# Decayed attention with two row buffers and decay products first in each gap; last pass shared by VectorE and GpSimd

## The chip, the cores and the metric

One core of one Trainium2 chip runs the whole program in one launch. The metric is the device time of one execution in microseconds, as the median of several. A core has TensorE (PE in the rows; PEld is its weight load), VectorE (DVE), ScalarE (ACT), GpSimd (POOL) and SyncE (SP), each with a queue of its own that is worked off in order; they wait for each other by semaphores.

## The reference

Four layers work on x of 8 x 512 tokens of width 256. After each layer comes `x = layernorm(x + layer(x))`, without gain or offset.

1. Softmax attention, 16 query heads, 4 key and value heads of 64, with rotary positions.
2. A feed-forward layer with quantized weights.
3. Decayed (linear) attention, 16 query heads over 4 key and value heads of 64, with rotary positions. Scores aren't put through a softmax. They are multiplied by a decay that depends on the head and on the distance of the tokens, and a state of 64 x 64 per head carries what lies before a chunk:

```
scores = einsum('bhtd,bhsd->bhts', qi, ki) * mask
o  = einsum('bhts,bhsd->bhtd', scores, vi) + einsum('bhtd,bhde->bhte', qi * q_dec, kv)
kv = blk_dec * kv + einsum('bhtd,bhte->bhde', ki * k_dec, vi)
```

4. A small attention, then a router that picks 2 of 8 experts for each token, and `x + 0.3 * (weighted sum of the two experts)` with the last layernorm behind it.

## The kernel before, in words

All arithmetic is float32. Where TensorE multiplies by weights, an operand is split into a high and a low part (`hi` and `lo`), and three products are summed.

*Decayed attention* (`decay_attention`, lines 640 to 1142) goes through the 8 batches in a loop. A batch has 512 tokens, four tiles of 128, and the kernel uses chunks of 256 tokens, two a batch. The steps of a batch are: transposes of x (`T`), VectorE's split of them (`XH`, `XL`, lines 965 and 969), projections (`Q`, `KV`, line 110), rotation (`ROT`, line 979, on VectorE, which writes two products side by side into the row buffer `rt`; `Y0` and `Y1`, line 1111, on GpSimd, which add them crosswise; `HI` and `LO`, lines 1116 and 1119, which split the sum into the stack `st`), transposes back (`QT`, `KT`, line 874), score products (`S`, line 893), their multiplication by the decay (`M`, line 1003, "decay product" here), the value product (`A`, lines 905 and 908), the state (`VD` on VectorE, line 992, into `vd`; `KV2` on TensorE, line 916; `KH`, a copy), its use (`IN`, line 924), its scaling and sum (`TM` and `OA`, lines 1009 and 1015), the split of the result (`HA` on ScalarE; `LA` on VectorE, line 1019, or on GpSimd, line 1130), the output projection (`W`, line 933), and the sum with x and the layernorm (`F`, `B`, `G`, `N`, lines 1026 to 1038, with `EPS` and `RSTD` on GpSimd, lines 1134 and 1139).

The order is written out by hand (lines 681 to 737). A round of 24 gaps holds one batch, and steps of the next batch lie ahead in it. `put(gap, engine, step)` places a step. Within a gap each engine's steps stand as they were put, but for a sort: TensorE by `turn`, ScalarE with `HA` first, VectorE with `F` first. A score product writes one of two PSUM banks, and waits until the decay product two before it has read that bank. In the first gap VectorE's order is `XH0 XL0 XH1 XL1 TM0 OA0 M`, and in gaps with a rotation the decay product stands behind it. A rotation (`ROT`) waits until GpSimd's `LO` of the rotation before has read `rt`. `VD` waits for the `KV2` of two groups before, as `vd` has two buffers.

*The last pass* (lines 2283 to 2363) comes when all expert tiles are written to memory. For each of 8 batches SyncE loads the two answers of every token (`y_part(b, 0)`, `y_part(b, 1)`, 128 x 1024 each) and x (`x_part(b)`). GpSimd adds the answers (line 2350), one batch ahead; VectorE makes 2x + sum (line 2287), then statistics (lines 2290 and 2295); GpSimd does four small operations on them (lines 2357 to 2363, `EPS`, the reciprocal root `rstd` by a power, shift and sign); ScalarE normalizes (line 2327) and issues the store.

Of the kernel before, what the change touches and what calls it, by code (L numbers as in the profile page):

```python
# [22 lines left out]
ALU = mybir.AluOpType  # L23
AX = mybir.AxisListType

P = 128
BATCH, SEQ, D = 8, 512, 256
TT = SEQ // P
KD = D // P
HEADS, KVH, HD = 16, 4, 64  # L30
GRP = HEADS // KVH
# [47 lines left out]
def shift(seq, n):  # L79

    return seq[0], seq[1] + n
# [551 lines left out]
def decay_attention(nc, const, x_in, x_out, w_q, w_kv, w_o, rope_tab, near_tab, from_tab, to_tab, name):  # L633
# [6 lines left out]
    with ctx:  # L640
        sb = lambda n, s, dt=F32: ctx.enter_context(nc.sbuf_tensor(f"{name}_{n}", s, dt))
# [3 lines left out]
        HH = HEADS // 2  # L645
# [9 lines left out]
        xth, xtl = (sb(n, [P, KD, SEQ], F32R) for n in ("xth", "xtl"))  # L655
        rt = sb("rt", [P, 2, HH * HD])
        kr = sb("kr", [P, 2, KVW])
# [3 lines left out]
        v = sb("v", [P, 2, TT, KVW])  # L661
        vd = sb("vd", [P, 2, 2, GRP * HD])
        kv = sb("kv", [P, 2, GRP * HD])
# [20 lines left out]
        gaps, ahead_keys = {}, {eng: set() for eng in ENGINES}  # L684
# [45 lines left out]
        for g in range(ROUND):  # L730
            gaps[g, "tensor"] = sorted(gaps.get((g, "tensor"), []), key=lambda k: -2 if k[0] == "W" and k[2] else turn[k[0]])
            gaps[g, "vector"] = sorted(gaps.get((g, "vector"), []), key=lambda k: k[0] != "F")
            gaps[g, "scalar"] = sorted(gaps.get((g, "scalar"), []), key=lambda k: k[0] != "HA")
# [5 lines left out]
        pe_s, dve_s, act_s, pool_s = (S[n] for n in ENGINES[:4])  # L739
# [4 lines left out]
        units = [k for k in order["tensor"] if k[0] in ("Q", "KV")]  # L744
        st_place = {("HI",) + k: n % 2 for n, k in enumerate(units)}
        rt_place = {("ROT",) + k: 0 for k in units}

# [31 lines left out]
        def rows_of(u):  # L779

            heads = HH if u[0] == "Q" else KVH
            line = kr[:, u[1], :] if u[0] == "KV" and u[1] < 2 else rt[:, 0, 0:heads * HD]
            stack = st[:, st_place[("HI",) + u], 0:heads * 2 * HD]
            return heads, line, line.rearrange("p (h d) -> p h d", d=HD), stack.rearrange("p (h d) -> p h d", d=2 * HD)

        with nc.Block() as block:
# [51 lines left out]
            def _(pe):  # L838
# [3 lines left out]
                def steps(i, run):  # L842
                    in_misc = [x for x in misc if x in run or x + (0,) in run]
                    for key in run:
                        kind, j = key[0], own(i, key)
# [8 lines left out]
                        if kind == "T":  # L854
                            k = key[1]
# [54 lines left out]
                        elif kind == "KV2":  # L910
# [3 lines left out]
                            for t in range(2):  # L914
                                for s in range(2):
                                    last = nc.tensor.matmul(m[HD * s:HD * s + HD, 0:GRP * HD], kr[:, t, HD * g:HD * g + HD], vd[:, g % 2, t, :], start=(t == 0), stop=(t == 1))
                        elif kind == "IN":
# [21 lines left out]
            def _(dve):  # L939
# [12 lines left out]
                def steps(i, run):  # L952
                    rot = [k for k in run if k[0] == "ROT"]
                    for key in run:
# [15 lines left out]
                        elif kind == "ROT":  # L970
# [5 lines left out]
                            for seq, k in last_use(i, rot, key, rt_place, ahead["vector"], order["vector"]):  # L976
                                dve.wait_ge(*pool_s.at(seq, "LO", *k[1:]))
                            w = heads * HD
                            op = vv.tensor_tensor(rt[:, :, 0:w].rearrange("p u (h d) -> p u h d", d=HD),  # L979
                                                  ps_m[:, bank[u], 0:w].rearrange("p (h d) -> p h d", d=HD).unsqueeze(1).broadcast_to([P, 2, heads, HD]),  # L980
# [6 lines left out]
                        elif kind == "VD":  # L987
                            g = key[1]
                            dve.wait_ge(*pool_s.at(j, "VV", 0))
                            dve.wait_ge(tables_in, 32)  # L990
                            dve.wait_ge(*(pe_s.at(j, "KV2", g - 2) if g >= 2 else pe_s.at(shift(j, -1), "KV2", g + 2)))
                            op = vv.tensor_tensor(vd[:, g % 2, :, :].rearrange("p t (h d) -> p t h d", d=HD),
                                                  v[:, 1, 0:2, HD * g:HD * g + HD].unsqueeze(2).broadcast_to([P, 2, GRP, HD]),
# [99 lines left out]
            def _(pool):  # L1093
# [3 lines left out]
                def steps(i, run):  # L1097
                    hi = [k for k in run if k in st_place]
                    for key in run:
                        kind, j = key[0], own(i, key)  # L1100
                        u = key[1:]
                        if kind in ("Y0", "Y1", "HI", "LO"):
                            heads, line, rows, stack = rows_of(u)
                            half = lambda x, c: x.rearrange("p (h c d) -> p h c d", c=2, d=HALF)[:, :, c, :]
                            a, b = rt[:, 0, 0:heads * HD], rt[:, 1, 0:heads * HD]
                        if kind in ("Y0", "Y1"):
# [907 lines left out]
def sparse_experts(nc, const, x_in, by_expert, answers, bias_parts, counts, raw, staged, w, x_out, name):  # L2014
# [6 lines left out]
    with ctx:  # L2021
# [70 lines left out]
        with nc.Block() as block:  # L2092
# [120 lines left out]
            def _(dve):  # L2213
# [69 lines left out]
                for b in range(BATCH):  # L2283
                    x = b % RAW
                    dve.wait_ge(staged[x], 16 * (len(pieces) // RAW) + 16 * (b // RAW) + 16)
                    dve.wait_ge(added, b + 1)
                    vv.scalar_tensor_tensor(out=y_part(b, 1), in0=x_part(b), scalar=2.0, in1=y_part(b, 0), op0=ALU.mult, op1=ALU.add).then_inc(summed, 1)
                    dve.wait_ge(summed, b + 1)
                    for t in range(TT):
                        vv.bn_stats(st6[:, b % 2, t, :], y_part(b, 1)[:, D * t:D * t + D]).then_inc(stats, 1)  # L2290
                    if b >= 2:
                        dve.wait_ge(normed, TT * (b - 1))
                    for t in range(TT):
                        hold(dve, stats, TT * b + t + 1)
                        vv.bn_aggr(mv[:, b % 2, t, :], st6[:, b % 2, t, :]).then_inc(means, 1)
# [37 lines left out]
            def _(pool):  # L2333
# [19 lines left out]
                for b in range(BATCH):  # L2353
                    if b + 1 < BATCH:
                        add(b + 1)
# [116 lines left out]
```

## Time and profile before

| | us |
|---|---|
| median of 3 runs | 3228.32 (3227.73 to 3229.99) |
| profiled execution | 3231.17 |
| its span | 3229.4 |
| TensorE busy | 2767.0 (86%) |
| VectorE busy | 1985.2 (61%) |
| ScalarE busy | 1299.3 (40%) |
| GpSimd busy | 1068.6 (33%) |

The span is what the profile of one execution shows, from its first to its last instruction. Decayed attention fills about 1450 to 2127 us of it, the last pass 3170 to the end. The mean granted clock of TensorE over the span is 0.942 of full speed. In a row, "idle before" is how long the engine did nothing ahead of that instruction, and the arrow names what ended it. Columns of the views are named at their first group below.

### The profile page before, as it was taken

What the parts mean: (1) busy time and instruction counts of PE and PEld (TensorE: products, weight loads), DVE (VectorE), ACT (ScalarE), POOL (GpSimd) and SP (SyncE); (2) the same over time, 40 slices, a digit from 0 to 9 for tenths busy, and PEclk for the clock granted to TensorE, in tenths of its full rate; (3) what the DMA queues carried; (4) which work ended last, traced back from release to release, by engine and by line L of the source; (5) the groups of instructions that cost most, each with busy time, mean ns of one, the idle gap of its engine ahead of it and who ended that gap; (6) DMA issues with size and microseconds to landing.
All of it is one profiled execution on the core that took longest, in us unless ns stands there. A gap on an engine that the chain in (4) does not pass through costs nothing. (4 is left out here: it accounts for less than half of the span.)

```text
span 3229.4 us, 62896 instructions
## 1 busy us (share of the span) xinstructions
PE 2767.0 (86%) x17098; PEld 1956.6 (61%) x17099; DVE 1985.2 (61%) x3659; ACT 1299.3 (40%) x2735; POOL 1068.6 (33%) x1446
## 2 busy tenths in 40 slices
PE   6998989999898978877999999969999999809992
PEld 4666666666675647765666666644555555408992
DVE  3656666565666658864555555557777777546664
ACT  2554554545454532212222222215555555424443
POOL 4333343434334311115555555510111111122225
PEclk8999999999999989999999999979999999959996
DMA  2111011111101121112111110022222222052225
GB/s 64 34 31 41 28 38 41 27 38 27 44 24 38 34 80 33 39 70 72 33 32 32 32 32 26 26 67 75 70 65 63 64 64 64 18 172 87 72 74 199
DMA packets 146409, 175.43 MB, mean 54 GB/s; under 512 B 21130, under 2 KB 109730, under 8 KB 145570
## 3 DMA queue, kind: packets, MB, share of 16 engines
q1 hardware_dynamic: 135076, 149.89, 15.9%
q0 software_dynamic: 6912, 18.96, 1.6%
q10 hardware_dynamic: 4224, 4.19, 0.4%
q8 instruction: 94, 1.54, 0.2%
q14 instruction: 103, 0.84, 0.1%
HBM read 90.83 MB, written 37.06 MB: 40 GB/s over the span
## 5 line engine op out<-in xcount | busy, mean ns | idle before, releaser
L560 ACT ACTIVATE soft_probs<-soft_ps_s,soft_mx 128x512 f32<-128x512 f32 x512 | 347.8, 685 | 395.1 <-DVE soft_mx L479 370.4
L479 DVE TENSOR_REDUCE soft_mx<-soft_ps_s 128x1 f32<-128x512 f32 x512 | 329.4, 685 | 236.7 <-PE soft_ps_s L389 224.1
L1817 DVE TENSOR_REDUCE mla_mx<-mla_ps_s 128x1 f32<-128x512 f32 x512 | 334.9, 686 | 133.7 <-PE mla_ps_s L1670 133.2
L1928 ACT ACTIVATE mla_pt<-mla_ps_t 128x512 f32<-128x512 f32 x512 | 289.9, 596 | 265.2 <-PE mla_ps_t L1682 263.1
L389 PE MATMUL soft_ps_s<-soft_ks,soft_qs 128*128 128x512 f32 x1024 | 309.8, 422 | 13.9 <-ACT soft_probs L560 13.9
L398 PE MATMUL soft_ps_p<-ident,soft_probs 128*128 128x128 f32 x2048 | 266.4, 273 | 12.0 <-DVE soft_mx L479 8.5
L398 PEld LDWEIGHTS soft_ps_p<-ident,soft_probs 128*128 128x128 f32 x2048 | 236.7, 141 | 46.7 <-DVE soft_mx L479 10.6
L489 DVE COPY soft_pt<-soft_ps_p 128x512 f32<-128x512 f32 x256 | 175.6, 686 | 138.7 <-PE soft_ps_p L398 134.0
L389 PEld LDWEIGHTS soft_ps_s<-soft_ks,soft_qs 128*128 128x128 f32 x1024 | 171.2, 190 | 147.9 <-issue 59.0
L407 PE MATMUL soft_ps_a<-soft_pt,soft_v 128*64 128x512 f32 x1024 | 251.2, 612 | 0.0
L1670 PE MATMUL mla_ps_s<-mla_stack,mla_pad 128*128 128x512 f32 x512 | 239.4, 474 | 8.8 <-DMA mla_pad<-mla_stack 5.9
L1682 PE MATMUL mla_ps_t<-mla_shifted,mla_pad 128*128 128x512 f32 x512 | 207.1, 407 | 0.2
L979 DVE TENSOR_TENSOR decay_rt<-decay_ps_m,decay_rope 128x1024 f32<-128x1024 f32 (+1 forms) x96 | 100.3, 1045 | 164.1 <-PE decay_ps_m L110 89.9
L567 ACT COPY soft_pt<-soft_ps_p 128x512 f32<-128x512 f32 x256 | 149.8, 585 | 83.0 <-PE soft_ps_p L398 72.3
L1692 PE MATMUL mla_ps_a<-mla_pt,mla_v 128*32 128x256 f32 x2048 | 168.5, 402 | 12.6 <-ACT mla_pt L1928 12.5
L1670 PEld LDWEIGHTS mla_ps_s<-mla_stack,mla_pad 128*128 128x128 f32 x512 | 100.2, 196 | 129.8 <-DVE mla_mx L1817 85.3
L1111 POOL TENSOR_TENSOR decay_rt<-decay_rt 128x256 f32<-128x256 f32 (+1 forms) x160 | 115.1, 740 | 156.3 <-DVE decay_rt L979 156.3
L893 PE MATMUL decay_ps_s<-decay_qs,decay_ks 128*128 128x512 f32 x384 | 138.2, 441 | 32.7 <-DVE decay_pt L1003 32.7
L588 POOL TENSOR_TENSOR soft_rt<-soft_rt 128x256 f32<-128x256 f32 (+1 forms) x192 | 120.2, 648 | 136.5 <-DVE soft_rt L466 136.5
L1067 ACT CAST decay_qs<-decay_ps_m 128x512 fp32r<-128x512 f32 x128 | 70.2, 589 | 185.0 <-PE decay_ps_m L874 184.4
L2344 POOL DMA_INDIRECT answers<-moe_blank,moe_xt x72 | 69.1, 960 | 227.7 <-DVE moe_blank L2265 227.7
L466 DVE TENSOR_TENSOR soft_rt<-soft_ps_m,soft_rope 128x1024 f32<-128x1024 f32 (+1 forms) x96 | 99.6, 1038 | 71.9 <-POOL soft_st L599 38.9
(359 smaller groups left out, 6577.9 us busy)
## 6 DMA issues: line engine op xcount, KB each, us to landing
soft_rrep<-inverse SPq DMA_DIRECT2D x128, 128.0 KB, 2.9
mla_pad<-mla_stack SPq DMA_DIRECT2D x256, 64.0 KB, 2.0
moe_xt<-by_expert SPq DMA_DIRECT2D x72, 129.0 KB, 2.0
soft_ks<-soft_ks SPq DMA_DIRECT2D x64, 128.0 KB, 2.3
decay_ks<-decay_ks SPq DMA_DIRECT2D x64, 128.0 KB, 2.4
raw<-in_L_ffn_w SPq DMA_DIRECT2D x16, 512.0 KB, 5.4
mla_stack<-mla_yh SPq DMA_DIRECT2D x128, 64.0 KB, 2.1
soft_xc<-in_L_attn_x SPq DMA_DIRECT2D x8, 512.0 KB, 4.3
```

The costliest lines, as they stand in the source:

```text
L389: last = nc.tensor.matmul(ps_s[:, s_bank(n), :], qs[:, h, P * t:P * t + P], ks[:, b, g, :], start=(b == 0), stop=(b == 1))
L398: last = nc.tensor.transpose(ps_p[:, c % 2, P * t:P * t + P], probs[:, h % 2, t, P * c:P * c + P], ident[:, :])
L407: last = nc.tensor.matmul(ps_a[HD * s:HD * s + HD, 0, :], v[:, 1, c, HD * g:HD * g + HD], weights_of(2 * p + s, c), start=(c == 0), stop=( ...
L479: op = vv.tensor_reduce(out=mx[:, h, t:t + 1], in_=ps_s[:, s_bank(4 * h + t), :], axis=AX.X, op=ALU.max, negate=True)
L489: op = vv.tensor_copy(weights_of(h, c), ps_p[:, c % 2, :])
L560: op = nc.scalar.activation(probs[:, h % 2, t, :], ps_s[:, s_bank(4 * h + t), :], ACT.Exp, bias=mx[:, h, t:t + 1], scale=1.0, accum_out=rs ...
L567: op = nc.scalar.copy(weights_of(h, c), ps_p[:, c % 2, :])
L1670: last = nc.tensor.matmul(ps_s[:, (4 * t + s + 16 * a) % S_BANKS, :], pad[:, QUADS + a, s, P * t:P * t + P], stack[:, a, :], start=True, s ...
L1682: last = nc.tensor.matmul(ps_t[:, s % 2, :], pad[:, a, s, P * t:P * t + P], shifted[:, a, :], start=True, stop=True)
L1692: last = nc.tensor.matmul(ps_a[32 * s:32 * s + 32, 0, cols], v[:, t, 4 * a + s, :], pt[:, t % 2, s, cols], start=(t == 0 and half == 0), s ...
L1817: op = vv.tensor_reduce(out=mx[:, a, t, s:s + 1], in_=ps_s[:, (16 * a + 4 * t + s) % S_BANKS, :], axis=AX.X, op=ALU.max, negate=True)
L1928: op = nc.scalar.activation(pt[:, t % 2, s, :], ps_t[:, s % 2, :], ACT.Exp, scale=KPH ** -0.5)
```

## The change

- The row buffer `rt` gets two places. Rotations take them in turn, and each waits for GpSimd's `LO` of the rotation before the last. `vd` goes from two buffers to one, and `VD` waits for the `KV2` of the group just before.
- On VectorE the sort within a gap puts decay products (`M`) first, then `F`, then the rest as put.
- In the last pass GpSimd adds the answers of even batches only. For odd batches VectorE makes 2x + first answer, and then adds the second answer.

```
-        rt = sb("rt", [P, 2, HH * HD])
+        rt = sb("rt", [P, 2, 2, HH * HD])
-        vd = sb("vd", [P, 2, 2, GRP * HD])
+        vd = sb("vd", [P, 2, GRP * HD])
-            gaps[g, "vector"] = sorted(gaps.get((g, "vector"), []), key=lambda k: k[0] != "F")
+            gaps[g, "vector"] = sorted(gaps.get((g, "vector"), []), key=lambda k: {"M": 0, "F": 1}.get(k[0], 2))
-        rt_place = {("ROT",) + k: 0 for k in units}
+        rt_place = {("ROT",) + k: n % 2 for n, k in enumerate(units)}
...
-                            dve.wait_ge(*(pe_s.at(j, "KV2", g - 2) if g >= 2 else pe_s.at(shift(j, -1), "KV2", g + 2)))
+                            dve.wait_ge(*(pe_s.at(j, "KV2", g - 1) if g else pe_s.at(shift(j, -1), "KV2", KVH - 1)))
...
-                    dve.wait_ge(added, b + 1)
-                    vv.scalar_tensor_tensor(out=y_part(b, 1), in0=x_part(b), scalar=2.0, in1=y_part(b, 0), op0=ALU.mult, op1=ALU.add).then_inc(summed, 1)
-                    dve.wait_ge(summed, b + 1)
+                    if b % 2 == 0:
+                        dve.wait_ge(added, b // 2 + 1)
+                        vv.scalar_tensor_tensor(out=y_part(b, 1), in0=x_part(b), scalar=2.0, in1=y_part(b, 0), op0=ALU.mult, op1=ALU.add).then_inc(summed, 2)
+                    else:
+                        dve.wait_ge(tile_in[b], DONE + 32)
+                        vv.scalar_tensor_tensor(out=y_part(b, 0), in0=x_part(b), scalar=2.0, in1=y_part(b, 0), op0=ALU.mult, op1=ALU.add).then_inc(summed, 1)
+                        dve.wait_ge(summed, 2 * b + 1)
+                        vv.tensor_tensor(y_part(b, 1), y_part(b, 0), y_part(b, 1), ALU.add).then_inc(summed, 1)
+                    dve.wait_ge(summed, 2 * b + 2)
...
-                    if b + 1 < BATCH:
+                    if b % 2 and b + 1 < BATCH:
                         add(b + 1)
```

## Rows read from the trace of the kernel before

**Rows 1.** Stretches: bounds, length, busy PE PEld DVE ACT POOL, granted clock, DMA.

```profile
1430.00:2127.00 697.00, 617.85 (x3997) 444.38 (x3995) 391.86 (x618) 143.65 (x259) 362.08 (x499) 0.96 0.13 39
...
1769.80:1773.20 3.40, 3.40 (x24) 2.25 (x22) 0.00 (x0) 1.17 (x2) 0.00 (x0) 0.76 0.00 0
```

**Rows 2.** Waits of PE in 1540:2100: total, times, longest.

```profile
PE decay_ps_s L893 <- DVE decay_pt L1003: 25.4, 25, 2.1
PE decay_ps_m L933 <- POOL decay_atl L1130: 9.5, 7, 1.4
```

**Rows 3.** Waits of DVE in 1540:2100.

```profile
DVE decay_rt L979 <- POOL decay_st L1119: 44.4, 33, 2.4
```

**Rows 4.** Timeline of PE: start, us, what, count, [idle before, releaser]; round's start.

```profile
1764.04 0.66 PE L874 MATMUL decay_ps_m<-ident,decay_st 128*128 128x128 f32 x4 [0.72 <-DVE decay_xtl L969]
1764.45 0.71 PE L893 MATMUL decay_ps_s<-decay_qs,decay_ks 128*128 128x512 f32 x2
1767.28 0.74 PE L893 MATMUL decay_ps_s<-decay_qs,decay_ks 128*128 128x512 f32 x2 [2.12 <-DVE decay_pt L1003]
1767.95 1.08 PE L905 MATMUL decay_ps_a<-decay_pt,decay_v 128*64 128x256 f32 x4
...
1769.38 1.97 PE L874 MATMUL decay_ps_m<-ident,decay_st 128*128 128x128 f32 x8
1771.28 0.93 PE L916 MATMUL decay_ps_m<-decay_vd,decay_kr 128*64 128x256 f32 x6
```

**Rows 5.** Timeline of DVE at the round's start.

```profile
1760.56 1.23 DVE L979 TENSOR_TENSOR decay_rt<-decay_ps_m,decay_rope 128x1024 f32<-128x1024 f32 x1 [2.37 <-POOL decay_st L1119]
...
1762.57 0.69 DVE L965 CAST decay_xth<-decay_ps_m 128x512 fp32r<-128x512 f32 x1 [0.19 <-PE decay_ps_m L859]
...
1766.55 0.68 DVE L1003 TENSOR_TENSOR decay_pt<-decay_ps_s,decay_near 128x512 f32<-128x512 f32 x1
1767.15 0.68 DVE L992 TENSOR_TENSOR decay_vd<-decay_v,decay_from_end 128x512 f32<-128x512 f32 x1
```

**Rows 6.** Timeline of PE, score products in 1776:1788.

```profile
1780.75 0.73 PE L893 MATMUL decay_ps_s<-decay_qs,decay_ks 128*128 128x512 f32 x2 [0.84 <-DVE decay_pt L1003]
...
1785.67 0.74 PE L893 MATMUL decay_ps_s<-decay_qs,decay_ks 128*128 128x512 f32 x2 [0.91 <-DVE decay_pt L1003]
```

**Rows 7.** Timeline of PE in 1812:1826.

```profile
1815.98 1.04 PE L874 MATMUL decay_ps_m<-ident,decay_st 128*128 128x128 f32 x8
...
1817.40 0.65 PE L905 MATMUL decay_ps_a<-decay_pt,decay_v 128*64 128x256 f32 x4
...
1823.10 0.38 PE L933 MATMUL decay_ps_m<-decay_woh,decay_ath 128*128 128x256 f32 x1 [1.36 <-POOL decay_atl L1130]
```

**Rows 8.** Timeline of DVE in 1812:1826.

```profile
1816.06 0.67 DVE L1038 TENSOR_SCALAR decay_xb<-decay_xb,decay_mv,decay_rstd 128x256 f32<-128x256 f32 x1 [1.58 <-POOL decay_rstd L1139]
1816.66 1.21 DVE L979 TENSOR_TENSOR decay_rt<-decay_ps_m,decay_rope 128x1024 f32<-128x1024 f32 x1
```

**Rows 9.** Timeline of POOL at the round's start.

```profile
1767.46 1.50 POOL L1130 TENSOR_TENSOR decay_atl<-decay_ot,decay_ath 128x512 fp32r<-128x512 f32 x1 [1.76 <-ACT decay_ath L1087]
```

**Rows 10.** Timeline of DVE, the next round's first cast.

```profile
1845.17 0.69 DVE L965 CAST decay_xth<-decay_ps_m 128x512 fp32r<-128x512 f32 x1 [0.20 <-PE decay_ps_m L859]
```

**Rows 11.** Timeline of POOL in the last pass.

```profile
3209.28 2.35 POOL L2350 TENSOR_TENSOR moe_w1h<-moe_w1h,moe_w1l 128x1024 f32<-128x1024 f32 x1
...
3212.13 1.75 POOL L2359 TENSOR_TENSOR moe_rstd<-moe_vare,minus_half 128x4 f32<-128x4 f32 x1 [0.18 <-POOL moe_vare L2357]
...
3214.65 2.35 POOL L2350 TENSOR_TENSOR moe_w1h<-moe_w1h,moe_w1l 128x1024 f32<-128x1024 f32 x1
...
3220.72 1.04 POOL L2359 TENSOR_TENSOR moe_rstd<-moe_vare,minus_half 128x4 f32<-128x4 f32 x1 [0.18 <-POOL moe_vare L2357]
```

**Rows 12.** Timeline of DVE in the last pass, one batch.

```profile
3211.74 1.24 DVE L2287 SCALAR_TENSOR_TENSOR moe_w1l<-moe_w2h,moe_w1h 128x1024 f32<-128x1024 f32 x1 [2.36 <-POOL moe_w1h L2350]
```

**Rows 13.** Stretch near the end of the last pass's loads.

```profile
3208.00:3210.00 2.00, 0.00 (x0) 0.00 (x0) 1.38 (x8) 0.64 (x2) 1.63 (x4) 0.50 0.83 291
```

More of the change, by code:

```diff
@@ L781, in rows_of @@
             heads = HH if u[0] == "Q" else KVH
-            line = kr[:, u[1], :] if u[0] == "KV" and u[1] < 2 else rt[:, 0, 0:heads * HD]
+            line = kr[:, u[1], :] if u[0] == "KV" and u[1] < 2 else rt[:, rt_place[("ROT",) + u], 0, 0:heads * HD]
             stack = st[:, st_place[("HI",) + u], 0:heads * 2 * HD]
@@ L915, in steps @@
                                 for s in range(2):
-                                    last = nc.tensor.matmul(m[HD * s:HD * s + HD, 0:GRP * HD], kr[:, t, HD * g:HD * g + HD], vd[:, g % 2, t, :], start=(t == 0), stop=(t == 1))
+                                    last = nc.tensor.matmul(m[HD * s:HD * s + HD, 0:GRP * HD], kr[:, t, HD * g:HD * g + HD], vd[:, t, :], start=(t == 0), stop=(t == 1))
                         elif kind == "IN":
@@ L978, in steps @@
                             w = heads * HD
-                            op = vv.tensor_tensor(rt[:, :, 0:w].rearrange("p u (h d) -> p u h d", d=HD),
+                            op = vv.tensor_tensor(rt[:, rt_place[key], :, 0:w].rearrange("p u (h d) -> p u h d", d=HD),
                                                   ps_m[:, bank[u], 0:w].rearrange("p (h d) -> p h d", d=HD).unsqueeze(1).broadcast_to([P, 2, heads, HD]),
@@ L990, in steps @@
                             dve.wait_ge(tables_in, 32)
-                            dve.wait_ge(*(pe_s.at(j, "KV2", g - 2) if g >= 2 else pe_s.at(shift(j, -1), "KV2", g + 2)))
-                            op = vv.tensor_tensor(vd[:, g % 2, :, :].rearrange("p t (h d) -> p t h d", d=HD),
+                            dve.wait_ge(*(pe_s.at(j, "KV2", g - 1) if g else pe_s.at(shift(j, -1), "KV2", KVH - 1)))
+                            op = vv.tensor_tensor(vd[:, :, :].rearrange("p t (h d) -> p t h d", d=HD),
                                                   v[:, 1, 0:2, HD * g:HD * g + HD].unsqueeze(2).broadcast_to([P, 2, GRP, HD]),
@@ L1104, in steps @@
                             half = lambda x, c: x.rearrange("p (h c d) -> p h c d", c=2, d=HALF)[:, :, c, :]
-                            a, b = rt[:, 0, 0:heads * HD], rt[:, 1, 0:heads * HD]
+                            place = rt_place[("ROT",) + u]
+                            a, b = rt[:, place, 0, 0:heads * HD], rt[:, place, 1, 0:heads * HD]
                         if kind in ("Y0", "Y1"):
```

## The prediction

> **What bounds the kernel now.** I read the page's slices first, then the stage of decayed attention by stretches, then who waits for whom in it, then one of its rounds engine by engine, and last the pass that ends the kernel. A round is one pass of the stage's loop. It can be timed by the first VectorE cast of a batch: 1762.57 us in one round [rows 5], 1845.17 in the next [rows 10], so 82.6 us. In the stage TensorE is busy 617.85 of 697 us, VectorE 391.86 and GpSimd 362.08 [rows 1]: TensorE sets its length, and only what leaves TensorE idle, or slows its clock, can give time. In the 560 us of six round starts TensorE waited 25.4 us for VectorE's decay products (25 times, the longest 2.1) and 9.5 us for GpSimd's low half of the result (7 times) [rows 2]. The waits of VectorE itself, 44.4 us of rotations for GpSimd [rows 3], cost nothing by themselves. They cost where a decay product stands in VectorE's queue behind them.
>
> One round shows where. (a) The score product at 1767.28 waits 2.12 us [rows 4], because its PSUM bank is freed by a decay product that runs seventh in its gap, at 1766.55, behind two casts, two subtractions, one scaling and one sum that began at 1762.57 [rows 5]. TensorE's work right behind it is slow: four matmuls of 256 columns take 1.08 us where they else take 0.65, eight transposes 1.97 where they else take 1.04 [rows 4, 7]. There the granted clock is 0.76 on the mean of a stretch [rows 1], so it fell to the lower level (1.2 GHz) for a part of it, after the round's longest idle. (b) Two more score products wait 0.84 and 0.91 us for decay products that stand behind rotations [rows 6]. (c) The output projection of tile 2 waits 1.36 us for GpSimd [rows 7].
>
> In the last pass GpSimd is the queue that never rests: per batch an addition of 2.35 us, then four small operations that fill the 3.0 us until the next addition [rows 11]. A batch costs 5.37 us (3209.28 to 3214.65). VectorE and ScalarE idle half of it.
>
> **Part 1: decay products first in each gap (and two row buffers).** No instruction is added, and no duration changes. What changes is order.
>
> At (a) the product at 1766.55 goes ahead of the casts. Its scores were made before the transposes of x, and the queue is free for it: the rotation that now starts at 1760.56 after a wait of 2.37 us for GpSimd [rows 5] no longer waits with a second buffer, and the product behind that one goes ahead of it too. So the casts still start at 1762.57, when their transposes are there, and I cost their delay at nothing (if that cover were missing, 0.6 us, one product). The bank is free early, and TensorE goes on behind the score product of 1764.45: next score product at about 1765.05, value product at 1765.7, transposes at 1766.5 (from start to start 0.67 us as at 1767.28, and 0.8 us for the eight matmuls of a value product), done at 1767.3. Next late are the decayed values `vd`: their multiplication starts where it does now, at 1767.15, and ends at 1767.83 [rows 5], so the state matmuls start at 1767.9 after 0.6 us of idle. They start at 1771.28 now [rows 4]. Of these 3.4 us, the slow clock makes (1.97 - 1.04) + (1.08 - 0.65) and a little more of the same value product [rows 4, 7], about 1.7; the order alone makes 1.7.
>
> At (b) both waits go, 0.84 + 0.91 = 1.75 us [rows 6]. The product that frees the bank for 1785.67 needs the scores begun at 1780.75, 4.9 us earlier, so it has them well before the rotation that now stands ahead of it; the other place is alike. Where a product runs behind a rotation and TensorE doesn't wait, the new order gives nothing.
>
> At (c) the order costs. The chain is: reciprocal root on GpSimd, normalization on VectorE at 1816.06 (it waited 1.58 us for that), rotation at 1816.66 [rows 8], GpSimd's four operations on it, its low half of the result, and then TensorE at 1823.10 [rows 7]. A decay product now steps between normalization and rotation: plus 0.6 us on a path that TensorE waits for. The second row buffer doesn't help here, since the normalization came last, not the buffer.
>
> Sum for a round: 1.7 + 1.75 - 0.6 = 2.85 us. Seven batches are overlapped with a next one and have all these places, so 20 us. Bounds: if nothing but (b) comes, 7 x (1.75 - 0.6) = 8; if the 0.6 us at (c) isn't paid, 7 x 3.45 = 24.
>
> **The clock.** With the idle of 2.12 us gone, the stretch ahead of the fall holds idles of 0.7 and 0.6 us instead of 0.72 and 2.12, and a score and a value product between them. Idles like that occur elsewhere in the round ((b), (c)) and no fall follows them. Nothing in the trace shows where the line is, so I bound it: 0 if it still falls each round, 7 x 1.7 = 12 if it never falls. I take 8, five rounds of seven without it.
>
> **Part 2: one buffer less for `vd`, the buffers themselves.** Each multiplication into `vd` now waits for the state matmuls of the group before, not of two before. In TensorE's order those matmuls stand ahead of scores whose decay product VectorE has to do before that multiplication anyway, so the wait is over when it is reached. Nothing; if it were on the path, about one group of state matmuls, 0.93 us [rows 4], a round. The second row buffer takes most of VectorE's 44.4 us of waits [rows 3] away. What that gives TensorE is in (a) already: the queue is free early there.
>
> **Part 3: the last pass.** Per two batches GpSimd loses one addition (2.35 us), VectorE gains one product of 1.24 us [rows 11, 12] and its queue for an odd batch has two of them in a row. The cycle that ends last is then: addition for the even batch, VectorE's product and statistics on it (3.0 us), GpSimd's small operations on it, next addition. The small operations last 3.0 us when one VectorE product runs beside them; the root takes 1.75 us beside it and 1.04 alone [rows 11]. Beside two products in a row they last between 3.0 and 4.3. A pair costs 8.5 to 9.8 instead of 10.74. Batches 1 to 6 take 30.6 us now, from statistics to statistics (6 x 5.37 less the part of an addition that is ahead at the start, 1.6), and 3 pairs, 25.5 to 29.4, then. Batch 7 takes two products and statistics, 4.25 us, instead of 5.37. So its root, at 3220.72 now [rows 11], comes 2.3 to 6.2 us earlier. A second bound: the loads still keep the DMA engines 0.83 busy in 3208 to 3210 [rows 13], so batch 7 is not there before about 3209.5, later if the stores come earlier. That cuts the top to about 5. I take 3.5.
>
> The Trainium skill (SBUF — State Buffer, section "Who interferes with whom") says that a VectorE instruction with two SBUF inputs and a GpSimd instruction that reads SBUF exclude each other, and that whichever starts first holds the port for the whole instruction. The root's 1.75 against 1.04 us [rows 11] agrees for the order in which VectorE is first. By that rule alone the long end of the pair, 9.8 us, would hold, and the pass would give 2.3 us instead of 3.5. The same rule speaks against part 1 at one place, which is rival 3.
>
> **Sum.** 20 + 8 + 3.5 = 31.5 us. The profiled execution took 3231.17 us (span 3229.4 and 1.8 around it), 2.9 above the median of the runs, 3228.32. From 3231.17 it gives 3199.7, and as a median 3197.
>
> **Rivals.**
> 1. *The clock still falls each round.* For it: it falls in all rounds now, whatever the length of the rest, and the transposes around 1762 to 1764 stay. Against: the long idle is what this place has and the others don't. Then 20 + 3.5: 3205.
> 2. *The waits move instead of going.* TensorE arrives earlier at rotations' transposes and at GpSimd's results. For it: GpSimd's chain already holds TensorE at (c), VectorE's casts hold it 0.72 us [rows 4]. Against: only 9.5 us of TensorE's waits are for GpSimd's results now [rows 2], so most of them come early. If (b)'s gains are given back and the clock stays as it is, 7 x (1.7 - 0.6) + 3 = 11: 3217.
> 3. *The multiplication into `vd` gets behind GpSimd's subtraction.* They start 0.3 us apart, VectorE first (1767.15 and 1767.46) [rows 5, 9]. If GpSimd were first by a little and VectorE had to wait for its 1.5 us, the state matmuls would start 1.2 us later each round: 8 us less gain, 3205. (The Trainium skill's same section makes this a full block.)
> 4. *Slower.* A decay product in front of every rotation puts 0.6 us before each of the 12 rotations of a round. It decides from the point where GpSimd's lead over the transposes is under 0.6 us: at (c) there is none now. If the lead were gone at all twelve, 7.2 us a round would be lost against 3.9 of idle removed (2.12 + 1.75): 7 x 3.3 less 3.5, 20 us slower: 3248. With half of them it comes out level.
> 5. *The order doesn't do what it says.* The score products would wait for something else (a state copy, a bank of the projections). Then only part 3: 3225.
>
> **How the numbers follow.** Forecast (31.5 us) 0.50; rival 1 0.24; rival 3 or mixtures with rival 1 0.07; rival 2 0.09; rival 5 0.04; rival 4 0.06. A measurement of this kernel tells about 0.2% (6.5 us) from no change. Faster by more than that: 0.50 + 0.24 + 0.07 + 0.09 = 0.90. Within: 0.04 and a part of rival 4, 0.05. Slower: 0.05. The likeliest case alone spans 3187 (24 + 12 + 5) to 3203 (20 + 2 + 3). The range with rivals 1 and 3 and a part of 2 is 3186 to 3213.
>
> **What would show it.** Right: no score product waits over 0.3 us for a decay product; the state matmuls start within 5.5 us of a batch's first cast (8.7 now); rounds of 78 to 80; no rotation waits for GpSimd; the wait at (c) about 2 us; the batches of the last pass 4.3 to 4.9 us apart. Clock: pieces of 8 transposes of 1.97 us missing. Wrong: rounds above 81 us, or a new releaser of the score products.

## The result and the profile after

| | before | after |
|---|---|---|
| median of 4 runs, us | 3228.95 (3227.73 to 3229.99) | 3178.57 (3169.70 to 3181.52) |
| profiled execution, us | 3231.17 | 3180.66 |
| its span | 3229.4 | 3178.9 |
| mean granted clock | 0.942 | 0.945 |

The ratio is 0.9833, 95% interval 0.9821 to 0.9846: 50 us less. The forecast was 3197, range 3186 to 3213. The sign was right, and so was what was said of the places in a round and of the last pass. The gain was put too low, mainly by what the second row buffer gives, and the time lies 7 us under the range.

The stretches show where the time is. The first row answers to [rows 1]; the second and third are one round each, from the first cast of a batch to that of the next. Columns as there.

```profile
1430.00:2080.00 650.00, 601.40 (x4020) 442.73 (x4019) 401.50 (x619) 142.22 (x259) 363.29 (x500) 0.98 0.14 42
1663.72:1740.90 77.18, 73.58 (x498) 54.08 (x497) 49.18 (x77) 17.18 (x32) 44.97 (x62) 1.00 0.12 34
1740.90:1818.03 77.13, 73.54 (x498) 54.08 (x497) 49.20 (x76) 17.18 (x32) 44.97 (x62) 1.00 0.12 34
```

A round took 82.5 to 83.9 us before, 83.02 on the mean of six, and takes 77.2 now. The granted clock is 1.00 in each of them. In the kernel before the clock fell to its lower level (1.2 GHz) once in every round, and two kinds of rounds stood beside each other: a round with the longer fall has a mean granted clock of 0.96, the common one 0.98 (same view):

```profile
1678.76:1762.57 83.81, 77.16 (x498) 55.43 (x497) 48.23 (x77) 17.39 (x32) 44.96 (x63) 0.96 0.11 31
1762.57:1845.17 82.60, 75.94 (x498) 54.84 (x497) 48.11 (x77) 17.38 (x32) 44.96 (x63) 0.98 0.11 32
```

From SyncE's first load of x in decayed attention to its last store of x, right behind the last normalization, it is 695.3 us before (1442.5 to 2137.8) and 642.6 after (1444.3 to 2086.9): 52.7 less. The six rounds make 35.1 of it, what lies before the second batch 6.0 (71.1 to 65.1), what lies behind the last batch's first cast 11.6 (126.1 to 114.5). The last pass is 3.1 shorter. Two other stretches, which the change doesn't touch, are together 5.3 longer: 1.8 ahead of decayed attention, 3.5 between it and the last pass.

The waits of TensorE after, in the six rounds, answer to [rows 2] (total, times, longest):

```profile
PE decay_ps_m L933 <- POOL decay_atl L1131: 10.9, 7, 1.6
PE decay_ps_m L874 <- DVE decay_xtl L969: 4.3, 6, 0.7
PE decay_ps_m L874 <- POOL decay_st L1120: 3.2, 7, 0.5
PE decay_ps_m L916 <- DVE decay_vd L992: 3.1, 6, 0.5
PE decay_ps_m L933 <- DVE decay_rt L979: 2.3, 7, 0.3
```

The waits for decay products, 25.4 us before, are gone. Two new waits have come, on `vd` and on a rotation at the output projection (L933). VectorE's side answers to [rows 3]:

```profile
DVE decay_pt L1003 <- PE decay_ps_s L893: 84.0, 68, 2.9
```

The direction has turned round: the decay products now wait for scores. The waits of rotations for GpSimd, 44.4 us before, are 2.6, in 5 times, the longest 0.5. The round's start, TensorE, answers to [rows 4]:

```profile
1742.78 1.17 PE L893 MATMUL decay_ps_s<-decay_qs,decay_ks 128*128 128x512 f32 x4
1743.88 0.65 PE L905 MATMUL decay_ps_a<-decay_pt,decay_v 128*64 128x256 f32 x4
...
1744.68 1.09 PE L874 MATMUL decay_ps_m<-ident,decay_st 128*128 128x128 f32 x8
1746.29 1.08 PE L916 MATMUL decay_ps_m<-decay_vd,decay_kr 128*64 128x256 f32 x8 [0.51 <-DVE decay_vd L992]
```

Both score products run in one piece (x4, no wait), the four value matmuls take 0.65 us instead of 1.08, and the eight transposes 1.09 instead of 1.97. The state matmuls start 5.4 us behind the first cast (1740.90), 8.7 before. At (c) the order costs what was forecast. VectorE there, which answers to [rows 8]:

```profile
1788.47 0.67 DVE L1038 TENSOR_SCALAR decay_xb<-decay_xb,decay_mv,decay_rstd 128x256 f32<-128x256 f32 x1 [1.58 <-POOL decay_rstd L1140]
1789.07 0.68 DVE L1003 TENSOR_TENSOR decay_pt<-decay_ps_s,decay_near 128x512 f32<-128x512 f32 x1
1789.67 1.21 DVE L979 TENSOR_TENSOR decay_rt<-decay_ps_m,decay_rope 128x1024 f32<-128x1024 f32 x1
```

And TensorE, which answers to [rows 7]:

```profile
1796.10 0.38 PE L933 MATMUL decay_ps_m<-decay_woh,decay_ath 128*128 128x256 f32 x1 [1.57 <-POOL decay_atl L1131]
```

### The profile page after: what moved, and what is told of

Its sections match the earlier page's. It is cut to its first block and busy times, and to the rows that moved or that the text cites. A ratio compares the mean times of both kernels' runs of the same rounds, so it can differ in the third digit from the quotient of the medians.

```text
span 3178.9 us, 62892 instructions
## 1 busy us (share of the span) xinstructions
PE 2753.1 (87%) x17098; PEld 1955.3 (62%) x17099; DVE 1998.0 (63%) x3663; ACT 1297.7 (41%) x2735; POOL 1062.3 (33%) x1442
## 5 line engine op out<-in xcount | busy, mean ns | idle before, releaser
L1003 DVE TENSOR_TENSOR decay_pt<-decay_ps_s,decay_near 128x512 f32<-128x512 f32 x192 | 131.0, 686 | 100.5 <-PE decay_ps_s L893 99.0
L1693 PE MATMUL mla_ps_a<-mla_pt,mla_v 128*32 128x256 f32 x2048 | 169.3, 404 | 12.7 <-ACT mla_pt L1929 12.7
L614 POOL CAST soft_ath<-soft_ot 128x512 fp32r<-128x512 f32 x64 | 39.1, 611 | 305.6 <-DVE soft_ot L495 301.6
```

What stands on the lines that cost most here:

```text
L1693: last = nc.tensor.matmul(ps_a[32 * s:32 * s + 32, 0, cols], v[:, t, 4 * a + s, :], pt[:, t % 2, s, cols], start=(t == 0 and half == 0), s ...
```

## The experiments

The kernels ran on several chips, whose medians of the kernel before lie between 3229 and 3261 us. Totals are therefore compared as ratios within one chip, and the parts by the length of a round, which on all of them repeats within 0.2 us when the clock does the same. A fall is a stretch at the lower level of the clock, and "clock falls" counts the rounds that have one.

| kernel | ratio to before (95%) | round, us | clock falls in six rounds |
|---|---|---|---|
| before | 1 | 82.5 to 83.9 | 6 |
| buffers alone | 0.9947 (0.9928 to 0.9966) | 81.7 | 6 |
| order alone | 0.9890 (0.9871 to 0.9910) | 78.1 | 0 |
| last pass alone | 0.9997 (0.9985 to 1.0008) | 81.1 once, else 82.5 to 84.0 | 5 |
| without the last pass | 0.9853 (0.9832 to 0.9875) | 77.2 | 0 |
| changed | 0.9833 (0.9821 to 0.9846) | 77.2 | 0 |
| first gap only | 0.9874 (0.9857 to 0.9890) | 77.7 | 0 |
| all but the first gap | 0.9943 (0.9929 to 0.9956) | 80.5 and 81.9 | 6 |
| rotation first in gap 16 | 0.9821 (0.9808 to 0.9835) | 76.6 | 0 |
| LA first | 0.9797 (0.9783 to 0.9810) | 75.4 | 0 |
| product after the casts | 0.9857 (0.9841 to 0.9873) | 77.7 | 0 |
| product before the sum | 0.9866 (0.9849 to 0.9883) | 78.2 and 79.7 | 2 |
| combined | 0.9764 (0.9750 to 0.9777) | 74.0 | 0 |
| last pass, all on VectorE | 0.9837 (0.9823 to 0.9850) | 77.2 | 0 |

### The four parts

**The buffers alone.** The changed kernel with the last pass of before and the old sort:

```
-            gaps[g, "vector"] = sorted(gaps.get((g, "vector"), []), key=lambda k: {"M": 0, "F": 1}.get(k[0], 2))
+            gaps[g, "vector"] = sorted(gaps.get((g, "vector"), []), key=lambda k: k[0] != "F")
```

> The buffers alone (two row buffers, one vd), with the old order in each gap and the old last pass. Theory A (the order of the decay products is the cause; the buffers only empty VectorE's queue): in the first gap the decay product still stands behind two casts and two subtractions, so the score product there still waits about 2 us, the clock still falls each round, rounds stay at 81 to 83 us; the 44 us of rotations that wait for GpSimd go; 0 to 8 us faster than before: 3221 to 3229. Theory B (the rotations' waits for GpSimd were what held the decay products behind them; the second row buffer is the cause): both waits of (b), 0.84 and 0.91 us, go and rounds shorten by 2 us or more: 3200 to 3215.

Neither theory held. It is 17 us faster than before. TensorE still waits 2.1 us at (a) and the clock still falls, as A said, but rounds are 0.9 us shorter than the common ones before, and none has the longer fall. Of (b)'s two waits the one of 0.84 is gone, as B said, and the one of 0.91 stays. And the first batch, which has no other batch's work beside it, is 4.4 us shorter (62.80 to 58.38). The two stretches, the first batch and one round:

```profile
1451.47:1509.85 58.38, 45.98 (x245) 33.03 (x246) 30.95 (x39) 14.92 (x23) 37.26 (x49) 0.87 0.31 104
1591.56:1673.30 81.74, 75.92 (x498) 54.92 (x497) 48.03 (x77) 17.38 (x32) 44.96 (x63) 0.98 0.12 32
```

Why the first batch gains is seen in VectorE's waits. The kernel before in 1440 to 1515:

```profile
DVE decay_rt L979 <- POOL decay_st L1119: 20.7, 8, 4.1
```

The buffers alone in 1438 to 1512:

```profile
DVE decay_rt L979 <- PE decay_ps_m L110: 21.0, 10, 6.4
```

There a rotation waited up to 4.1 us for GpSimd, and TensorE, which has no other batch's work there, waited too: 2.2 us for rotations and 7.8 for the stacks that GpSimd makes of them, against none and 6.2 with two row buffers. Rotations then wait for their projections only.

**The order alone.** The kernel before with the new sort:

```
-            gaps[g, "vector"] = sorted(gaps.get((g, "vector"), []), key=lambda k: k[0] != "F")
+            gaps[g, "vector"] = sorted(gaps.get((g, "vector"), []), key=lambda k: {"M": 0, "F": 1}.get(k[0], 2))
```

> The order alone (decay products first in each gap), with one row buffer, two vd and the old last pass. Theory A: score products stop waiting for decay products, the clock stops falling, rounds of about 77 to 78 us as in the changed kernel; rotations go on waiting for GpSimd (about 44 us) at no cost: 38 to 47 us faster than before, 3182 to 3190. Theory B: without the second buffer the waits of rotations hold the decay products, score products go on waiting 15 us or more in 1540 to 2060, 10 to 25 us faster: 3204 to 3218.

Theory A holds for the clock and the score products: none waits, and the rounds are 78.06. But by the ratio it is 35 us faster than before, less than the 38 to 47 of A, and the waits of rotations for GpSimd do have a cost: a round is 0.9 us longer than with the buffers, and the first batch takes 63.0 us, as before. First batch and one round:

```profile
1446.43:1509.43 63.00, 45.80 (x245) 31.75 (x246) 31.32 (x39) 14.97 (x23) 35.73 (x48) 0.89 0.29 97
1743.62:1821.68 78.06, 73.95 (x498) 54.05 (x497) 48.70 (x77) 17.28 (x32) 45.02 (x63) 1.00 0.12 34
```

In the rounds TensorE has a wait that neither the kernel before nor the changed one has (its waits in 1540 to 2060):

```profile
PE decay_ps_m L874 <- DVE decay_rt L979: 3.2, 6, 0.5
```

Its place in the timeline of TensorE:

```profile
1766.71 0.66 PE L874 MATMUL decay_ps_m<-ident,decay_st 128*128 128x128 f32 x4 [0.54 <-DVE decay_rt L979]
```

And the rotation that it waits for, in that of VectorE:

```profile
1765.43 1.23 DVE L979 TENSOR_TENSOR decay_rt<-decay_ps_m,decay_rope 128x1024 f32<-128x1024 f32 x1 [2.19 <-POOL decay_st L1119]
```

The rotation `Q01` stands 2.19 us at GpSimd's `LO`, and while it stands its PSUM bank of the projections stays full; the transposes `QT001` need a bank. In the changed kernel the same rotation starts 2.4 us earlier in the round, and the eight transposes run in one piece. All later steps of the round are then 0.7 to 0.9 us earlier.

**The last pass alone.** The kernel before with the last pass of the changed one (its diff stands above, under the change).

> The last pass alone, decayed attention as before. Both theories: 3.1 us faster than before (what the two profiles differ by from the last gather's start to the last store), 3225. If the changed pass only looks faster because it comes at another point of the loads, 0 to 1 us.

The medians differ by 2.3 us and the interval of the ratio holds 1, so the total alone doesn't tell it. The trace does: from the start of the last indirect DMA of answers (the "gather" of the expectation) to the last store it is 51.3 us, 54.2 before and 51.1 in the changed kernel. This run also gave by chance what no planned one could, the price of the clock. Its first round kept the full clock, with all waits of the kernel before in it. Three rounds:

```profile
1514.88:1595.98 81.10, 74.42 (x498) 53.85 (x497) 48.13 (x77) 17.28 (x32) 45.01 (x63) 1.00 0.12 34
1595.98:1679.88 83.90, 77.26 (x498) 55.45 (x497) 48.17 (x76) 17.38 (x32) 44.97 (x63) 0.96 0.11 31
1679.88:1762.51 82.63, 76.00 (x498) 54.86 (x497) 48.11 (x76) 17.37 (x32) 44.96 (x63) 0.98 0.11 32
```

TensorE at the start of the first of them, with the same long idle and quick matmuls behind it:

```profile
1519.58 0.73 PE L893 MATMUL decay_ps_s<-decay_qs,decay_ks 128*128 128x512 f32 x2 [2.11 <-DVE decay_pt L1003]
1520.24 0.65 PE L905 MATMUL decay_ps_a<-decay_pt,decay_v 128*64 128x256 f32 x4
```

So a fall costs 1.5 us (82.63 - 81.10), and the longer kind 2.8 (83.90 - 81.10). The kernel with the product before the sum, below, has the first price again (79.77 against 78.24). Before, four rounds of six had the first and two the second: 1.92 us a round (83.02 - 81.10).

**The changed kernel without its last pass.** The edit is the one of the last pass alone, taken back.

> The changed kernel with the old last pass. If the parts add up: 3.1 us slower than the changed kernel, 3182, 47 us faster than before. Then the order alone (the run beside it) and this one differ by what the buffers give beside the order: under 3 us by theory A, 20 us or more by theory B.

The parts add up: by its ratio it is 47 us faster than before, as forecast, with rounds of 77.2 and a first batch of 57.8. From the order alone (0.9890) to this one (0.9853) the buffers give 0.37%, 12.6 us by the medians. Runs of one kernel lie up to 12 us apart here, so the medians alone are rough, but the stretches say the same: 6 x 0.88 in the rounds, 5.2 in the first batch and 2.6 in the last make 13.1. That is neither under 3, as theory A had it, nor over 20.

### The places in the round

**Decay products first in the first gap only.**

```
-  key=lambda k: {"M": 0, "F": 1}.get(k[0], 2))
+  key=lambda k: {"M": 0, "F": 1}.get(k[0], 2) if g == 0 else k[0] != "F")
```

> The changed kernel with decay products first in the first gap of a round only (the other gaps in the old order). Theory A (the places are separate; the long idle at the first gap is what makes the clock fall): no clock fall in the rounds, no wait of 2.1 us there; the score-product wait of 0.91 us and the one of 0.18 come back, the 0.6 us at the output projection of tile 2 goes: rounds of 77.8 to 78.5 us (77.2 in the changed kernel, 81.7 with the buffers alone), 4 to 9 us slower than the changed kernel. Theory B (the clock falls by TensorE's idle over the whole round, and needs all of the order): falls come back, rounds of 79.5 or more, 16 us slower than the changed kernel.

Theory A holds, with rounds of 77.74 us just under its low end. TensorE's waits for decay products are 7.3 us in 13 times, the longest 0.9. By the ratios it is 13 us slower than the changed kernel, where 4 to 9 were said. The rounds give 0.57 each, and 5.0 lie behind the last batch's first cast (119.5 us against 114.5), of which more below.

**In all gaps but the first.**

```
-  key=lambda k: {"M": 0, "F": 1}.get(k[0], 2))
+  key=lambda k: {"M": 0, "F": 1}.get(k[0], 2) if g else k[0] != "F")
```

> The changed kernel with the old order in the first gap of a round only. Theory A: the score product there waits 2.1 us again, the clock falls once a round right behind it, the state matmuls start 8.7 us behind the first cast (5.4 in the changed kernel): rounds of 80.5 us, 23 us slower than the changed kernel. Theory B: the idle comes back but the clock stays up: rounds of 78.9 us, 12 us slower.

Theory A holds in kind: the wait of 2.1 us, a fall in each round, 80.55 us in two rounds with the short fall. It had no longer fall, and four rounds have one and take 81.8 to 81.9. So the kernel is 35 us slower than the changed one by the ratios (30 by the stretches), not 23. Against 77.2 that is 1.8 us of order and 1.5 or 2.8 of clock, in one gap.

**The rotation first in gap 16.**

```
-  key=lambda k: {"M": 0, "F": 1}.get(k[0], 2))
+  key=lambda k: {"M": 0, "F": 1}.get(k[0], 2) if g != 16 else k[0] != "F")
```

> The changed kernel with the rotation ahead of the decay product in the one gap where the normalization stands before them. By the price of the chain (one decay product of 0.6 us between them, on a path that TensorE waits for): the wait of the output projection of tile 2 goes from 1.57 to about 1.0 us, rounds of 76.6 us, 4 us faster than the changed kernel. If that wait is hidden by something else next, nothing.

Measured 76.55 to 76.61 a round, 0.6 less: the price of (c) was right, and nothing hides it. It doesn't all come where it was expected. The wait for `atl` goes from 1.57 to 1.36 only; the other 0.33 are the wait for a rotation at the projection's first half, which is gone.

**GpSimd's LA first.**

```
+            gaps[g, "gpsimd"] = sorted(gaps.get((g, "gpsimd"), []), key=lambda k: k[0] != "LA")
```

> The changed kernel with GpSimd's low half of the result (LA) first in each gap, so ahead of the four operations of a rotation. In the gap of the output projection of tile 2, GpSimd then does it in the 2.06 us in which it now waits for the rotation. The wait of 1.57 us goes: rounds of 75.6 us, 11 us faster than the changed kernel. Rival: the rotation's operations come 0.7 us later in five other gaps, and TensorE waits for their transposes: 0 to 5 us faster.

75.4 us a round, and 11.6 us faster than the changed kernel by the ratios. The wait for `atl` has left the list of TensorE's waits in the rounds. The rival is wrong. GpSimd had idled 2.06 us for the rotation with work that was ready standing behind it in its queue.

### How the clock hangs on the idle

Two kernels set the place of the decay product in the first gap: behind the two casts and their subtractions, or behind the scaling too.

```
-  key=lambda k: {"M": 0, "F": 1}.get(k[0], 2))
+  key=lambda k: {"M": 0, "F": 1}.get(k[0], 2) if g else {"XH": 0, "XL": 0, "M": 1}.get(k[0], 2))
...
+  key=lambda k: {"M": 0, "F": 1}.get(k[0], 2) if g else {"XH": 0, "XL": 0, "TM": 0, "M": 1}.get(k[0], 2))
```

> The changed kernel with the decay product of the first gap behind the two casts and two subtractions, ahead of the scaling and the sum: it ends about 3.3 us behind the first cast, and the score product that is ready at 2.5 us waits 0.8 to 0.9 us (0 in the changed kernel, 2.1 in the old order). A question of the clock. Theory A (the fall needs the long idle): granted clock 1.00 in all rounds, rounds of 77.2 us and up to 0.9 more, 77.5 to 78.1. Theory B (any idle there is enough, so the fall is one of place): it falls each round, 79.0 to 80.5.

The idle is 0.8 us, the clock falls in no round, and rounds take 77.74. TensorE there:

```profile
1663.87 0.73 PE L893 MATMUL decay_ps_s<-decay_qs,decay_ks 128*128 128x512 f32 x2 [0.80 <-DVE decay_pt L1003]
```

> The same with the decay product one place later, behind the scaling: the score product waits 1.4 to 1.6 us. Theory A: somewhere between 0.9 and 2.1 us of idle the fall sets in; if it is not here, rounds of 78.1 to 78.8 us at clock 1.00; if it is, 1.5 us more (what a round with a fall cost in the kernel with the last pass alone, 82.6 against 81.1 us), 79.6 to 80.3, or both kinds of rounds mixed.

The idle is 1.4 us, and both kinds of rounds stand beside each other, as the last case of A said. TensorE in a round without a fall:

```profile
1666.93 0.73 PE L893 MATMUL decay_ps_s<-decay_qs,decay_ks 128*128 128x512 f32 x2 [1.40 <-DVE decay_pt L1003]
```

Two rounds of the kernel with the product before the sum:

```profile
1504.93:1584.70 79.77, 75.34 (x498) 54.97 (x497) 49.02 (x76) 17.37 (x32) 45.00 (x63) 0.98 0.12 34
1584.70:1662.94 78.24, 73.79 (x498) 54.00 (x497) 49.02 (x77) 17.28 (x32) 44.91 (x62) 1.00 0.12 34
```

So at this one place of the round: falls in 0 of 6 rounds with an idle of 0.8 us, 2 of 6 with 1.4, and 23 of 24 with 2.1 (the kernel before, the buffers alone, the last pass alone, all but the first gap). With none, as in the changed kernel, 0 of 6. The length of one idle doesn't decide it everywhere: at (c) the changed kernel idles 1.57 us in each round, longer than the 1.4 here, and no fall follows. What else counts wasn't tested.

### Two attempts to go further

**Combined.** LA first, the rotation first in gap 16, and two moves in the first gap:

```
-        for g, at in enumerate((12, 14, 22, 25)):
-            put(at, "vector", ("VD", g)); put(at + 1, "tensor", ("KV2", g)); put(at + 1, "scalar", ("KH", g))
+        for g, at in enumerate((12, 14, 22, 24)):
+            put(at, "vector", ("VD", g)); at += g == 3; put(at + 1, "tensor", ("KV2", g)); put(at + 1, "scalar", ("KH", g))
...
+        first = gaps[0, "tensor"]
+        first.insert(first.index(("QT", 1, 2, 1)), first.pop(first.index(("S", 1, 1, 2))))
```

> A version meant to beat both. The changed kernel with GpSimd's LA first in each gap (75.4 us a round by itself), the rotation ahead of the decay product in gap 16 (the output projection's first half then stops waiting 0.33 us for it), the score product S112 between the two transposes that wait 0.72 us for a cast, and the multiplication VD3 one gap earlier, so that the state matmuls stop waiting 0.51 us. If the waits are separate: 75.4 - 0.33 - 0.72 - 0.51 = 73.8 us a round, 23 us faster than the changed kernel over seven batches. Rival: the scaling and sum behind the earlier multiplication come 0.6 us later and something behind them holds TensorE: 74.4 or more. If a new idle brings the clock down, 76 or more.

Forecast 73.8; 74.0 us a round, 3154.18 us where the kernel before takes 3230.18 and the changed one, by its own ratio, 3176: it beats both. Of TensorE's waits in 1540 to 2020 these two are left:

```profile
PE decay_ps_m L877 <- POOL decay_st L1123: 3.2, 7, 0.5
PE decay_ps_m L877 <- DVE decay_xtl L972: 1.6, 6, 0.3
```

**The last pass all on VectorE.** Each batch goes as the odd ones of the changed kernel:

```
-                    if b % 2 == 0:
-                        dve.wait_ge(added, b // 2 + 1)
-                        vv.scalar_tensor_tensor(out=y_part(b, 1), in0=x_part(b), scalar=2.0, in1=y_part(b, 0), op0=ALU.mult, op1=ALU.add).then_inc(summed, 2)
-                    else:
...
-                add(0)
...
-                    if b % 2 and b + 1 < BATCH:
-                        add(b + 1)
```

> The changed kernel with all additions of the last pass on VectorE (two products a batch, no GpSimd addition). If GpSimd's queue bounds the pass, and the second product only moves work off it: a batch takes VectorE 4.25 us, a pair 8.5 against 9.56 in the changed kernel, and the first batch starts 2.4 us earlier: last store 4 us earlier. Rival: the loads (DMA engines 0.83 busy almost to the last batch) don't keep up: 0 to 2 us.

The rival holds: from the last indirect DMA of answers to the last store it is 50.0 us, 1.2 less than in the changed kernel, and the total shows no difference from it (0.9837 and 0.9833). VectorE, with no GpSimd ahead of it, stands at the loads twice (its timeline):

```profile
3150.93 1.23 DVE L2288 SCALAR_TENSOR_TENSOR moe_w1h<-moe_w2h,moe_w1h 128x1024 f32<-128x1024 f32 x1 [1.79 <-DMA moe_w1l<-answers]
3157.03 1.23 DVE L2288 SCALAR_TENSOR_TENSOR moe_w1h<-moe_w2h,moe_w1h 128x1024 f32<-128x1024 f32 x1 [1.84 <-DMA moe_w1l<-answers]
```

The DMA engines are full meanwhile (column before the last, 1.09). They are as full in the changed kernel, 1.09 in 3130 to 3160, but there VectorE never stands at a load in this stretch:

```profile
3150.00:3155.00 5.00, 0.00 (x0) 0.00 (x0) 4.00 (x9) 2.65 (x6) 3.14 (x3) 0.50 1.09 384
```

## Why the prediction put the gain too low

| term | forecast | measured |
|---|---|---|
| order in the rounds, (a) to (c) | 7 x 2.85 = 20 | 7 x 3.04 = 21.3 |
| clock | 8 (at most 12) | 7 x 1.92 = 13.4 |
| the buffers | 0 | 12.7 |
| last batch, with no next one beside it | not counted | 4.1 |
| last pass | 3.5 | 3.1 |
| sum | 31.5 | 54.6 |

The 54.6, less 5.3 us by which the stretches outside the change are longer in this execution, are 49.3; the two profiled executions differ by 50.5. The 1.2 between lie at the start: 0.8 from the first load to the first cast, and 0.3 by which the first batch gained more than the mean that the table uses. Seven rounds are the six measured ones and the last overlapped batch, which is taken as alike.

**(a), (b), (c): right.** The order alone takes the rounds from 81.10 (full clock) to 78.06. The state matmuls start 3.3 us earlier, 3.4 forecast, and the new wait for `vd` is 0.51, 0.6 forecast. The stretch with (b)'s two waits is 2.1 us shorter, 1.75 forecast, and the place of the wait of 0.18 us, which the sum left out, gives 0.3. At (c) the loss is 0.59, 0.6 forecast. All signs named were met but three: rounds are 77.2 where 78 to 80 was said, the wait at (c) is 1.57 where 2 was, and rotations still wait 2.6 us for GpSimd where none should. (Batches of the last pass are 4.8 us apart on the mean of a pair, 5.4 and 4.2 singly.) Part of (c)'s loss shows as 0.33 us at the first half of the projection instead. The prediction priced the order together with the buffers. Taken so, a round without falls gains 3.9 us (81.10 to 77.2) where it said 2.85.

**The clock: the right mechanism, mis-sized.** The step "I take 8, five rounds of seven without it" failed twice. The clock falls in no round; no row stood behind five of seven. And the price of a fall, 1.7 us from the transposes and the value product of one round, left out that two rounds of six had a fall of twice the length: their rounds, 83.8 and 83.9 us against 82.6, stood in the trace of before, and the prediction timed one round only. So even its upper bound, 12, was under the 13.4 measured.

**The buffers: the step that was wrong.** It read "The second row buffer takes most of VectorE's 44.4 us of waits [rows 3] away. What that gives TensorE is in (a) already: the queue is free early there." The runs show three things in its place. 0.88 us a round (78.06 to 77.18), by the PSUM bank that a waiting rotation keeps full; seven times, 6.2. 4.9 us in the first batch (the mean of 4.4 without the order and 5.4 with it), where the rotations' waits are the path. And 1.7 in the last batch: what lies behind its first cast goes from 117.0 us with the order alone to 114.5, and one round's 0.88 is taken off. There TensorE waited 1.65 us for GpSimd's `LO` with one row buffer, and doesn't with two. The sum, before rounding, is 12.7. That the order alone creates the wait for the bank is rival 2 in small: the wait moved, and the buffer then took it.

**The last batch.** Order alone brings it from 126.1 to 117.0 us. Of the 9.1, a round's order and clock are 5.0, and 4.1 are beyond it. The kernel before waited 3.4 us for decay products in 2055 to 2140, three times, and its clock fell once more near the end. The wait:

```profile
PE decay_ps_s L893 <- DVE decay_pt L1003: 3.4, 3, 1.4
```

The stretch, with a granted clock of 0.64:

```profile
2129.00:2132.00 3.00, 3.00 (x19) 3.00 (x19) 1.03 (x3) 0.00 (x0) 0.22 (x1) 0.64 0.00 0
```

The prediction said "Seven batches are overlapped with a next one", counted those, and gave the batch without one nothing. The 4.1 belong to the gaps behind the first. The kernel with products first in the first gap only keeps two of these waits (0.82 and 1.43 us), a longer wait for `atl` (1.78 against 1.50) and a late fall (granted clock 0.66 in its 2083 to 2088), and takes 119.5 us behind the last batch's first cast. The changed kernel has none of them and takes 114.5. The kernel with the new order in all gaps but the first has neither these waits nor the late fall. How the 4.1 divide between the waits and the fall wasn't tested; the waits alone are 2.5.

**`vd`: right.** No wait of VectorE for the state matmuls stands among its waits. Rival 3 didn't come: GpSimd's subtraction starts at 1745.79, 0.31 us behind the multiplication (1745.48) and lasts 1.50, as before.

**The last pass: right.** Pairs of batches are 9.56 us apart (VectorE's product at 3143.31, 3152.87 and 3162.43), within 8.5 to 9.8 but near the long end, and the pass gives 3.1 us where 3.5 was taken. Two of GpSimd's rows beside VectorE's two products (3146.23 and 3147.49 us, 1.23 and 1.22 long) show why:

```profile
3146.49 1.04 POOL L2364 TENSOR_SCALAR moe_vare<-moe_mv 128x4 f32<-128x4 f32 x1 [0.24 <-DVE moe_mv L2302]
3147.72 1.89 POOL L2366 TENSOR_TENSOR moe_rstd<-moe_vare,minus_half 128x4 f32<-128x4 f32 x1 [0.18 <-POOL moe_vare L2364]
```

The first takes 0.23 us elsewhere and ends here at 3147.53, with VectorE's first product (3147.46); the root takes 1.04 alone, and here 1.89, to 3149.61, 0.90 behind the end of VectorE's second (3148.71). The Trainium skill (SBUF — State Buffer, "Who interferes with whom") says that whichever of the two issues first keeps the shared port for its whole instruction and the other is fully blocked. The first row agrees: it ends with the product. The second agrees nearly: it ends 0.90 us behind the product, where a root that began only then would take 1.04.

**The rivals.** The order alone excludes 1 (no fall) and 5 (no score product waits); 3 didn't come, as said of `vd`; 4 lost its 0.6 us at (c) alone. Of 2, a part was true of the order without the buffers: 0.88 us a round of waits that moved.

## What to carry to other kernels

A wait of an engine that isn't the bottleneck can cost more than the delay of what stands behind it in its queue: it keeps full the buffer that it has yet to read. So ask of each removed wait which PSUM bank comes free earlier and who needs it next. Price the first and the last iteration of a pipelined loop by themselves, since waits that are hidden in the middle are the path there; here they held 11 of the 23 us that the forecast lacked. Time several rounds before one is taken as the pattern, and when a round has one long idle of TensorE, count what the slow clock behind it costs as well.

## What the runs showed of the hardware

Whether the granted clock falls to its lower level (1.2 GHz) went by the idle at one place by degrees: none of 6 rounds behind 0.8 us, 2 of 6 behind 1.4, 23 of 24 behind 2.1. It is not the same in every round of one execution, and eight of these 23 falls were of the longer kind (2.8 us instead of 1.5). At another place of the round an idle of 1.57 us brought no fall in 6 rounds. An operation of 128x4 elements on GpSimd took 1.04 us instead of 0.23 when it started 0.26 us behind a VectorE product with two SBUF inputs, and ended with it.
